# Rotary feed-forward block: cosine products from PSUM, halved GpSimd sums, and a new order of exponentials and norm roots

## The reference, cut to what matters

```
def _layer(x, wqkv, qs, ksc, wo, lg, lb, w1, b1, w2, b2):
    h = shift_token(x)
    q, k, v = jnp.split(h @ wqkv, 3, axis=-1)         # 8 heads of 64
    q = l2norm(q) * qs
    k = l2norm(k) * ksc
    q, k = rotary_xpos(q, k)                          # q*cos*scale + rotate_half(q)*sin*scale
    o = local_attention(q, k, v)                      # windows of 64, softmax
    x = x + o @ wo
    h = layernorm(shift_token(x)) * lg + lb
    a, g = jnp.split(h @ w1 + b1, 2, axis=-1)
    return x + (a * gelu(g)) @ w2 + b2
```

## Time and profile before

| what | value |
|---|---|
| median of 3 runs (range) | 2468.51 us (2467.78 to 2474.09) |
| the profiled execution's own time | 2465.03 us |
| its span, first to last instruction | 2462.9 us |
| busy share: PE, DVE, ACT, POOL | 86%, 73%, 59%, 43% |
| mean granted TensorE clock over the span | 0.946 of full speed |

### The profile page before, as it was taken

How to read it: one execution, slowest core, us unless ns; L and a number is a source line. 1 busy time by engine, 2 the same in 40 slices (tenths; PEclk the granted TensorE clock), 3 DMA queues, 4 the chain that set the end, 5 groups by cost and what they waited for, 6 DMA issues and landing times. The chain is left out here.

```text
span 2462.9 us, 56322 instructions
## 1 busy us (share of the span) xinstructions
PE 2116.9 (86%) x23398; PEld 1565.7 (64%) x23398; DVE 1809.3 (73%) x2815; ACT 1462.6 (59%) x2389; POOL 1058.3 (43%) x800
## 2 busy tenths in 40 slices
PE   2799999998989868999868999999989997597968
PEld 1566666666666645555536667676666664495758
DVE  3688888888888646777727888888888884563556
ACT  0477776766666515666546776766666674363635
POOL 4665555545555210000035565655555450550245
PEclk8799999999999968999979999999999998698979
DMA  7000000079999995000000000000000003121122
GB/s 151 1 2 1 2 2 2 1 78 105 111 137 129 126 127 51 2 2 2 2 1 1 2 2 2 2 2 2 2 2 2 1 2 76 54 66 37 35 75 80
DMA packets 211376, 90.91 MB, mean 37 GB/s; under 512 B 79700, under 2 KB 206721, under 8 KB 210996
## 3 DMA queue, kind: packets, MB, share of 16 engines
q1 hardware_dynamic: 202596, 72.27, 24.5%
q0 software_dynamic: 6080, 11.76, 1.5%
q10 hardware_dynamic: 2448, 3.28, 0.6%
HBM read 24.31 MB, written 63.41 MB: 36 GB/s over the span
## 5 line engine op out<-in xcount | busy, mean ns | idle before, releaser
L490 POOL TENSOR_TENSOR work<-work,rot_tables 128x512 f32<-128x512 f32 x256 | 382.6, 1515 | 317.3 <-ACT work L594 317.3
L498 POOL TENSOR_TENSOR work<-work 128x1024 f32<-128x1024 f32 x128 | 304.8, 2381 | 283.6 <-DVE work L924 278.4
L941 DVE TENSOR_TENSOR work<-work,small 128x1024 f32<-128x1024 f32 x128 | 234.4, 1833 | 56.6 <-ACT small L608 50.1
L924 DVE TENSOR_TENSOR work<-work,rot_tables 128x1024 f32<-128x1024 f32 x128 | 219.3, 1713 | 11.6 <-ACT work L594 11.6
L1081 DVE TENSOR_REDUCE small<-psum 128x4 f32<-128x1024 f32 x128 | 156.6, 1223 | 90.3 <-PE psum L1582 88.5
L1482 PE MATMUL psum<-centered,ffn_w 128*128 128x256 f32 x768 | 191.2, 401 | 3.0 <-DVE centered L985 2.9
L705 ACT ACTIVATE work<-psum 128x1024 f32<-128x1024 f32 x128 | 131.0, 1024 | 88.7 <-PE psum L1582 88.4
L1323 PE MATMUL psum<-qkv_w_hi,h_hi 128*128 128x512 f32 x384 | 180.0, 469 | 2.2 <-ACT work L594 2.2
L1420 PE MATMUL psum<-work 64*128 64x128 f32 (+1 forms) x2048 | 178.9, 304 | 0.0
L1482 PEld LDWEIGHTS psum<-centered,ffn_w 128*128 128x128 f32 x768 | 146.0, 197 | 31.2 <-DVE centered L985 4.4
L1453 PE MATMUL psum<-work,v 128*32 128x192 f32 (+1 forms) x4096 | 164.8, 302 | 0.0
(11 more groups left out here) (279 smaller groups left out, 5266.1 us busy)
## 6 DMA issues: line engine op xcount, KB each, us to landing
h_area<-mean_weights SPq DMA_DIRECT2D x24, 2048.0 KB
tile_x<-h_area SPq DMA_DIRECT2D x39, 128.5 KB, 2.1
stage<-in_consts ACTq DMA_DIRECT2D x1, 2817.0 KB, 12.0
tile_x<-h_area SPq DMA_DIRECT2D x39, 64.5 KB, 1.8
work<-in_x SPq DMA_DIRECT2D x4, 512.0 KB, 27.2
expert_w<-in_ew SPq DMA_DIRECT2D x1, 2048.0 KB, 8.4
expert_w<-in_ew SPq DMA_DIRECT2D x8, 256.0 KB, 6.6
work<-y_tokens SPq DMA_DIRECT2D x4, 512.0 KB, 6.1
```

Of the source, the lines that this page charges most:

```text
L490: last = pool.tensor_tensor(b[:, :, :, o_], a[:, :, :, i_], tab[:, l, 1, t, :, o_].unsqueeze(2).to_broadcast([P, 2, HEADS, 32]), ALU.mult)
L498: pool.tensor_tensor(rC[:, t, :], rC[:, t, :], rB[:, t, :], ALU.add).then_inc(f_sum, 1)
L924: dve.tensor_tensor(g(rC[:, t, :]), g(rA[:, t, :]), tab[:, l, 0, t, :, :].unsqueeze(2).to_broadcast([P, 2, HEADS, DH]), ALU.mult)\
L941: dve.tensor_tensor(c_, c_, sm[0][:, 96 + 16 * t:112 + 16 * t].unsqueeze(2).to_broadcast([P, 16, DH]), ALU.mult).then_inc(f_nrm, 1)
```

## The change

Four edits, all within `ffn`. `cosines` takes its first input from PSUM and waits for the products (`f_qk`) instead of the copy; `copy_qk` now waits for `cosines` of the same tile, so that `f_cp` says that both are done with the banks. On VectorE `cosines(0)` moves up to between `k_out` and `resid`, and `cosines(1)` to right behind `y_normed`. On GpSimd `rotated` becomes two instructions of 128x512. On ScalarE `copy_v` goes ahead of `copy_qk(1)`, and two of the three `exps` go ahead of `rnorm`. On TensorE the wait for `f_cp` in `scores` moves to the masks of banks 0 and 1.

```diff
--- before.py
+++ after.py
@@ -495,7 +495,10 @@
                 def rotated(i, t):
                     pool.wait_ge(f_sin, 2 * i + t + 1)
                     pool.wait_ge(f_cos, 2 * i + t + 1)
-                    pool.tensor_tensor(rC[:, t, :], rC[:, t, :], rB[:, t, :], ALU.add).then_inc(f_sum, 1)
+                    for h in range(2):
+                        n_ = slice(h * INNER, (h + 1) * INNER)
+                        last = pool.tensor_tensor(rC[:, t, n_], rC[:, t, n_], rB[:, t, n_], ALU.add)
+                    last.then_inc(f_sum, 1)
 
                 def normed(s):
                     n = f * SEQS + s
@@ -587,8 +590,7 @@
 
             def ffn(f):
                 def copy_qk(i, t):
-                    act.wait_ge(f_qk, 3 * i + t + 1)
-                    free(act, f_cos, 2 * i + t - 1)
+                    act.wait_ge(f_cos, 2 * i + t + 1)
                     free(act, f_sin, 2 * i + t - 1)
                     src = PS[:, 1 + t:3 + t, :]
                     act.activation(rA[:, t, :].rearrange("p (b n) -> p b n", b=2), src, ACT.Copy).then_inc(f_cp, 1)
@@ -668,18 +670,20 @@
                         square(i - 2)
                         rstd(i - 2)
                     if new:
+                        copy_v(i)
                         copy_qk(i, 1)
-                        copy_v(i)
                         square_qk(i, 1)
                     if old:
                         gelu(i - 2)
                     if pre:
                         x_square(n)
+                    if mid:
+                        exps(i - 1, 0)
+                        exps(i - 1, 1)
                     if new:
                         rnorm(i)
                     if mid:
-                        for q in range(3):
-                            exps(i - 1, q)
+                        exps(i - 1, 2)
                     if mid:
                         recips(i - 1, 0)
                     if pre:
@@ -919,9 +923,9 @@
                 def cosines(i, t):
                     l, _ = layer_of(i)
                     g = lambda x: x.rearrange("p (g h d) -> p g h d", g=2, h=HEADS)
-                    dve.wait_ge(f_cp, 2 * i + t + 1)
+                    dve.wait_ge(f_qk, 3 * i + t + 1)
                     free(dve, f_qT, i)
-                    dve.tensor_tensor(g(rC[:, t, :]), g(rA[:, t, :]),
+                    dve.tensor_tensor(g(rC[:, t, :]), PS[:, 1 + t:3 + t, :].rearrange("p g (h d) -> p g h d", h=HEADS),
                                       tab[:, l, 0, t, :, :].unsqueeze(2).to_broadcast([P, 2, HEADS, DH]), ALU.mult)\
                         .then_inc(f_cos, 1)
 
@@ -1019,6 +1023,8 @@
                         o_norm(i - 2, 1)
                     if mid:
                         k_out(i - 1)
+                    if new:
+                        cosines(i, 0)
                     if old:
                         resid(i - 2)
                     if mid:
@@ -1032,12 +1038,11 @@
                     if old:
                         y_normed(i - 2)
                     if new:
-                        cosines(i, 0)
+                        cosines(i, 1)
                     if mid:
                         m_out(i - 1)
                     if new:
                         sums(i, 0)
-                        cosines(i, 1)
                     if old:
                         gated(i - 2)
                     if new:
@@ -1381,10 +1386,11 @@
                 def scores(i):
                     pe.wait_ge(f_kb, i + 1)
                     pe.wait_ge(f_qsb, i + 1)
-                    pe.wait_ge(f_cp, min(2 * i + 3, 2 * ITEMS * (f + 1)))
                     groups = (((3, 6), range(8), P, 0, 0, ms0), ((4, 5), range(4), J0W, 1, WIN, ms1),
                               ((0, 1), range(4, 8), J0W, 1, WIN, ms1))
                     for bs, hs, w, _, _, m in groups:
+                        if bs[0] == 0:
+                            pe.wait_ge(f_cp, min(2 * i + 3, 2 * ITEMS * (f + 1)))
                         bands(bs, len(hs) // 2, w, m)
                     for bs, hs, w, t, k0, _ in groups:
                         for h in hs:
```

## The result

After: 2551.57 us median of 4 runs (2548.58 to 2558.14). Before, beside it: 2468.85 us (2467.78 to 2474.09). The ratio is 1.0334, 95% interval 1.0308 to 1.036: 83 us slower, where 61 were forecast. The profiled execution took 2549.79 for a span of 2547.8, so 84.9 us of span came on.

The account below looks back on a forecast made before the run. Bound: a loop from VectorE through ScalarE's root pair, `qk_norm`, `resid2` and `o_norm(0)` to TensorE. 24 x 1.1 + 36 x 1.05 - 2 x 1.6 = 61 us, giving 2529 us; range 2488 to 2550.

Parts of the forecast that it names:

- items 1 to 6: Path through a short step, from the moved `cosines(0)` to `qk_norm(0)`; short and layer 1 steps +1.05 us each.
- item 3: VectorE's subtraction in `m_split` waits at the port for GpSimd's second half; `y_normed` 1.0 us later.
- the prediction's last sign: In the timeline after, a subtraction of `m_split` lasting 0.19 us would mean rival A.
- rival A: In `m_split` the subtraction doesn't wait; `y_normed` only 0.4 us late, +25 us, 2494 us; chance 0.16.
- item 4: ScalarE's copy of tile 1 waits for `cosines(1)`, then square, table load and GELUs; last `gated` 1.5 us later.
- B: VectorE stays the bound at the last `gated`, so its savings count; 2390 us at most; chance 0.09.
- C: No measurable change, if the path is 1 us shorter than added up; 2468 us; chance 0.05.
- Rival D: A further loss, such as TensorE's granted clock dropping; at +1.5 us a step, 2555 us; chance 0.05.
- item 7: Steps with an input norm: `x_square` ahead of the exponentials, `attend(0)` +0.9, `o_norm(0)` some 0.2 more; +1.1 us.
- Item 5: ScalarE runs two groups of exponentials before the root pair, which ends at 445.05; `attend(0)` comes 0.7 us later.
- item 6: On VectorE `qk_norm(0)` starts 2.6 us later but takes 1.23 instead of 2.71, ending 1.1 us late.

Follow-up runs that it names:

- after_rot_late: `after` with the GpSimd sum of tile 0 also waiting for `y_normed` of the same step; 2514.6 us.
- copy_first: `after_no_x` with tile 1 copied before its cosines, still read from PSUM, and `copy_qk(1)` ahead of `copy_v` again; 2431.8 us.
- after_resid: `after` with `resid2` ahead of `qk_norm(0)` on VectorE; 2525.1 us.
- before_h: The kernel before with only the GpSimd sums split in halves; 2458.7 us.
- tile0_h: `before_h` with the PSUM cosines, their earlier place, the copy behind them and the moved wait in `scores` for tile 0 only; 2433.8 us.
- after_no_x: `after` with all three groups of exponentials behind the norm roots again; 2526.5 us.
- before_x: The kernel before with only two groups of exponentials moved ahead of the norm roots; 2502.7 us.
- tile0_h_noclip: `tile0_h` without `clip`, a bias of 1e-15 in the logarithm replacing the lower bound; 2433.9 us.
- h_noclip: `before_h` without `clip`, a bias of 1e-15 in the logarithm replacing the lower bound; 2422.0 us.

## Why the prediction was right and wrong

**Right: items 1 to 6.** `cosines` from PSUM takes 1.217 us against the 1.22 taken. By the Trainium skill's larger fixed cost of a PSUM source (VectorE: DVE Perf Modes, the section on the TRN2 errata) an estimate would be 1.28; the extra does not show in this shape. The wait in `m_split` ends where item 3 put it (forecast 435.15 for the end of the subtraction with `proj` at 427.30; measured 435.17 with `proj` at 427.12), though it is the cast that stands still and not the subtraction behind it. By the letter of the prediction's last sign, a subtraction at 0.19, this would have been rival A; but the wait is there, one instruction earlier. Table load, GELUs, roots and `qk_norm(0)` all lie within 0.2 us of the forecast's clock. `after_rot_late` bears out the wait of item 3 (0.65 to 0.7 a step), `copy_first` item 4's mechanism, and short and layer 1 steps came out 0.06 and 0.07 below the forecast. Rivals A, B and C fell: the cast waits, and `gated` waits for ScalarE. Rival D, a further loss, came true by its time (2555 forecast, 2551.6 measured) but not by the cause that it names as its example: the granted clock stayed at 1.00 in every step that holds the extra loss.

**Wrong: item 7.** It says of steps with an input norm "`attend(0)`: +0.9. Then `o_norm(0)` is late by some 0.2 more. +1.1." Between `attend(0)` and `attend(1)` stands `x_var`, which may not write its half of bank 7 before `resid2` has read the other; item 7 puts that wait at nothing without naming it. The wait is in the code and was not in any row, since before `resid2` was done 0.43 us in time. Item 5 delayed the roots, item 6 `qk_norm(0)`, and `resid2` is queued behind it. Measured from `proj`, `resid2` ended 2.4 us later than before and `attend(0)` began only 1.1 later. TensorE stood 0.88 in each of these steps, and they cost 2.07 instead of 1.1: 24 x 0.97 = 23 us, which is what separates 61 from 84. `after_resid` shows it by removing it: its steps cost 1.15 over before. That the rest of item 7 comes to 1.1 is partly luck: `attend(0)` came 1.14 later instead of 0.9, and the 0.2 of `o_norm(0)` never appeared, since the transposes did not wait for it.

**What the parts cost.** From `before` to `before_h` -12 us, to `tile0_h` -25, to `after_no_x` +93, to `after` +25. The largest part, the +93, is the copy of tile 1 behind its cosines, which `copy_first` takes back. The expected gain went off the critical path: in a short step VectorE's 2.5 us of shorter instructions became 2.58 us of waiting for GELUs.

**Left open.** The uneven layer 1 steps of `before_x`; the 0.36 between `tile0_h_noclip` and `h_noclip`; and single steps 0.4 to 4.4 us longer than the rest about the middle of the first pass's layer 1, in ten of the fifteen traces (27.18 in `after`, 28.77 in `after_no_x`). Stores of constants to HBM run there, and in those two steps the granted clock was 0.97 and 0.94; which of this is cause was not tried.

## What to carry to other kernels

When two engines must read the same data one after the other, put first the one whose consumers are waiting; here a copy of 1.02 us, which ScalarE had to make before its GELUs, waited for a product that nobody needed yet, and turning the two gave back 95 us. When an instruction is delayed on purpose, list everything queued behind it and every engine that waits for that, waits of zero length in the old trace included. Look for tiny SBUF-to-SBUF instructions beside GpSimd: one of 0.18 us took 0.5 to 0.8 longer in every step. Keeping GpSimd back from the cast brought 37 us, and dropping the clip 37 in `before_h`, but nothing in `tile0_h`, where the clip met GpSimd hardly any more.

## What the runs showed of the hardware

A 128x32 cast with one SBUF input, not only instructions with two, stood still until the GpSimd instruction beside it had ended: 0.94 on average in `after`, 0.183 when GpSimd was kept away. The Trainium skill (SBUF — State Buffer, "Who interferes with whom") has casts among the VectorE instructions that can contend with GpSimd; the trace agrees. An addition with a scalar operand and two SBUF inputs was held up as well (1.92 for two instead of 0.85 in `h_noclip`). VectorE got its turn between two GpSimd instructions issued back to back: in `before_h` two halves took 3.58 instead of 2.5 with a product of 1.22 between them.
